# State-space phase of a four-layer kernel: smaller background products, at most one in a step

## The chip, the cores and the metric

The kernel runs on one core of one Trainium2 chip. The metric is the device time of one execution in microseconds (us), lower is better. The change touches the first of six phases, the program's first 4.49 ms.

## The reference, cut to what matters

The phase computes a 2-D selective state-space layer on four images of 48x48 positions and 128 channels: a layer norm, a projection to 2x256 channels, a depthwise 3x3 convolution with SiLU, four scans of the image (by rows and by columns, each forward and backward) and a gated projection back.

```python
xc = silu(conv3x3_depthwise(xc) + conv_b)            # 256 channels
xs = stack([x_hw, x_wh, x_hw[::-1], x_wh[::-1]])     # 4 orders of the 2304 positions
dts, Bs, Cs = split(x_proj_w @ xs)                   # 8 + 16 + 16 rows
delta = softplus(dt_w @ dts + dt_b)
# for each of 16 states n, along the positions t:
h = h * exp(delta_t * A[:, n]) + delta_t * u_t * B_t[n]
y_t += h * C_t[n]                                    # plus Ds * u
out = x + out_proj(layernorm(sum of 4 orders of y) * silu(z))
```

## The kernel before, in words

**Units and steps.** `layer0` (L112) cuts each of the 4 images x 4 passes into 5 chunks of 480, 480, 480, 480 and 384 positions. That makes 80 units (`units`), 20 to an image. In `units` an entry is (image b, o, d, chunk); o = 1 means that positions are read by columns, through a strided view. A unit has 16 steps, one for each state n, so the phase has 1280 steps g. Both halves of the 256 channels lie side by side, so one instruction does 2 x 480 elements.

**One order for all engines.** A planner in plain Python writes one list, `ph.order`, of named pieces of work. Each engine then walks this list and emits what is its own, in that order, with semaphore waits. So an engine never passes a piece that waits: whatever stands behind it waits too.

**The chain of a step.** For step g the list holds, in this order:

- `scan` g: VectorE's scan (L728), which needs `exp` g from ScalarE (L877, two halves; the second half of `exp` g+1 may start only when scan g has ended, since the three banks of `pA` are shared), `dbu` g from GpSimd (L941), and `add` g-4 (the buffer H has four places);
- `exp` g+1, and `carry` g (ScalarE, L885, waits for scan g);
- `c_spread` g-1 (TensorE): spreads row C of the state over 128 partitions in PSUM bank `pC`. There is one such bank, so it waits for `hc` g-2;
- `add` g-2 (TensorE, two products into `pY`). In the first step of a unit `add` waits until the previous unit's `pY` has been copied out (`y_out`, ScalarE, L894, put in step 1, right behind `add` of that unit's last step);
- `hc` g-1: VectorE's product of H with `pC` (L736), which needs `c_spread` g-1;
- `dbu` g+3 (GpSimd, up to three steps ahead).

**Work for the next unit.** `proj(u + 1)` is a Python generator; the loop advances it once in each step of unit u (`next(nxt, None)`). It puts `px` (TensorE, two products of 104 rows that give dts, B and C; ScalarE copies them out as `px_high` at L817 and `dts` at L821), `px_mid` and `px_low` (the rest of C's three bf16 parts), and for each half `dt`, `sp_exp`, `sp_ln`, `sp_max` and `du` (softplus; `sp_max` is VectorE's L719, `sp_ln` is ScalarE's L853 and L857). At step n = 12 (N - AHEAD - 1) whatever is left of it is put at once. `inject` (TensorE, step 9) adds the skip term or the earlier passes' sum into `pY`.

**Background work.** `todo` holds generators for other images: `front` (norm, the `in` and `z` products, the convolutions) and `back` (norm, gate and output projection of the image just finished). `further()` advances the first of them by one place. There is one place in a step, two in units 0 to 3 and, in the first pass of images 1 to 3 (`UB <= u and u % UB < 5`), two in every fourth step. A generator is held up where `take` finds neither of two free PSUM banks (`pM`), which `proj` and the background share. A convolution chunk of one channel half is nine TensorE products (taps), put as three pieces of three taps in three places (`conv` 0, 3, 6), then SiLU over five places. Where the chunk that the next unit reads is not ready (`ready_for`), the loop runs `further()` on the spot until it is.

The lines that matter: `take`, `conv`, `proj` and the step loop in the planner, L556 to L563 (`conv` on TensorE) and L589 to L596 (`px` on TensorE), L810 to L822 (`px` on ScalarE). All TensorE products share line L521 in the profile and are told apart by their tiles: `a_pC<-a_stk,a_sel` is `c_spread`, `a_pY<-a_H,cst` is `add`, `a_pM<-a_XC,a_w_x` is `px`, `a_pM<-a_xpad,a_cdiag` is `conv`, `a_pY<-a_Y,cst` is `inject` of a later pass. One fp32 product counts as two matmul instructions.

Of the kernel before, what the change touches and what calls it, by code (L numbers as in the profile page):

```python
# [111 lines left out]
def layer0(nc, A, X, K):  # L112
    ph = Phase(nc, "a")
# [105 lines left out]

    banks, freed, bank = [((), k) for k in range(8)], {}, {}  # L220

    def take(kind, *key):
        while not banks:
            yield
        freed[kind, key], bank[kind, key] = banks.pop(0)
        ph.put(kind, *key)

# [43 lines left out]
    def conv(b, h, c):  # L271
        yield from take("conv", b, h, c, 0)
        yield
        ph.put("conv", b, h, c, 3)
        yield
        ph.put("conv", b, h, c, 6)
        yield
        yield from silu("conv", b, h, c)
        give(("conv", (b, h, c, 0)), ("si_out", upto("si_out", "conv", b, h, c)))
        yield  # L280
# [52 lines left out]

    def proj(u):
        yield from take("px", u)
        ph.put("b_store", u)
        yield
        ph.put("px_mid", u)
        yield
        ph.put("px_low", u)  # L340
        give(("px", (u,)), ("px_low", u + 1))
        yield
        for h in range(2):
            k = 2 * u + h
            yield from take("dt", u, h)
            yield
            ph.put("sp_exp", u, h)
            yield
            ph.put("sp_ln", u, h)
            yield  # L350
            yield
            ph.put("sp_max", u, h)
            give(("dt", (u, h)), ("sp_max", k + 1))
            ph.put("du", u, h)
# [9 lines left out]

    def drain(target):
        for _ in target:
            pass

    def first_maps():
        yield from norm(0, 0, both)  # L370
# [16 lines left out]
    def further():  # L387

        while todo and next(todo[0], "end") == "end":
            todo.pop(0)  # L390
# [5 lines left out]
    def ready_for(u):  # L396

        b, o, d, ck = units[u]
        last = 4 if o or ck == 4 else ck
        return all(("si_out", ("conv", b, h, last)) in ph.rank for h in range(2))  # L400
# [13 lines left out]
    for g in range(G):  # L414
        u, n = divmod(g, N)
        if n == 0:
            b = u // UB
            if u % UB == 0:
                todo += ([back(b - 1)] if b else []) + ([front(b + 1)] if b + 1 < B else [])
            if u == NU - 5:  # L420
                todo.append(back(B - 1))
            if u + 1 < NU:
                while not ready_for(u + 1):
                    further()
            nxt = proj(u + 1) if u + 1 < NU else iter(())
        ph.put("scan", g)
        put_at("exp", g + 1)
        ph.put("carry", g)
        put_at("c_spread", g - 1)
        put_at("add", g - 2)  # L430
        put_at("hc", g - 1)
        put_at("dbu", g + AHEAD)
        if n == 1 and u:
            ph.put("y_out", u - 1)
        if n == 9:
            ph.put("inject", u)
        if (g + AHEAD) % 2:
            p = (g + AHEAD) // 2 + NB
            if p < G // 2:
                while ("b_store", (2 * p // N,)) not in ph.rank:  # L440
                    next(nxt)
                    further()
                ph.put("b_load", p)
        next(nxt, None)
        while n == N - AHEAD - 1 and next(nxt, "end") != "end":
            further()
        for _ in range(2 if u < 4 or UB <= u and u % UB < 5 and n % 4 == 3 else 1):
            further()
    ph.put("c_spread", G - 1)
    ph.put("add", G - 2)  # L450
# [1 line left out]
    ph.put("add", G - 1)  # L452
    ph.put("y_out", NU - 1)
    while todo:
        further()

    conv_ends = [key[:3] for kind, key in ph.order if kind == "conv" and key[3] == 6]
    conv_no = {key: k for k, key in enumerate(conv_ends)}

    def taken(kind, key):  # L460
# [18 lines left out]
    with nc.Block() as block:  # L479
# [38 lines left out]
        def _(pe):  # L518

            def mm(out, lhsT, rhs, start=True, stop=True):  # L520
                return pe.matmul(out, lhsT, rhs, start=start, stop=stop, skip_group_check=True)  # L521
# [11 lines left out]
            for kind, key in ph.order:  # L533
# [17 lines left out]
                elif kind == "conv":  # L551
# [4 lines left out]
                        wait_bank(kind, key)  # L556
                        pe.wait_ge(S("in_out"), upto("in_out", b, h, min(c + 1, 4)))
                    p = flat(taken("conv", (b, h, c, 0))[:, 0:z])
                    for t in range(t0, t0 + 3):
                        dy, dx = t // 3, t % 3  # L560
                        m = mm(p, cdiag[:, h, t, :], xpad[:, h, r0 + dy:r0 + dy + nr, dx:dx + 48], t == 0, t == 8)
                    if t0 == 6:
                        m.then_inc(S("conv"), 1)  # L563
                elif kind == "b_centre":
                    k = key[0]
# [23 lines left out]
                elif kind == "px":  # L589
# [3 lines left out]
                    for h in range(2):  # L593
                        pe.wait_ge(S("si_out"), upto("si_out", "conv", b, h, 4 if o else ck))
                    mm(p, w_x[:, 0, o + 2 * d, :], view(XC[:, b % 2, 0, :], o, ck), True, False)
                    mm(p, w_x[:, 1, o + 2 * d, :], view(XC[:, b % 2, 1, :], o, ck), False, True).then_inc(S(kind), 1)  # L596
                elif kind in ("px_mid", "px_low"):
                    u = key[0]
                    z = CHUNK[units[u][3]][1]
# [141 lines left out]
        def _(s):  # L741
# [4 lines left out]
            for kind, key in ph.order:  # L746
# [53 lines left out]
                elif kind == "b_rstd":  # L800
# [6 lines left out]
                    s.activation(rs[:, 0:BP], taken("b_var", key)[:, 0:BP], ACT.Ln, bias=K["eps5"]).then_inc(S("b_ln"), 1)  # L807
                    s.wait_ge(S("b_ln"), k + 1)
                    s.activation(rs[:, 0:BP], rs[:, 0:BP], ACT.Exp, scale=-0.5).then_inc(S(kind), 1)
                elif kind == "px":  # L810
                    u = key[0]
                    z = CHUNK[units[u][3]][1]
                    p = taken(kind, key)
                    s.wait_ge(S("px"), u + 1)
                    if u >= 2:
                        s.wait_ge(S("c_spread"), N * (u - 1))
# [2615 lines left out]
```

## Time and profile before

| | |
|---|---|
| three runs | 11725.56, 11732.56, 11735.66 us; median 11732.56 |
| profiled execution | 11683.06 us, span of its instructions 11681.3 us |
| mean granted TensorE clock | 0.936 of full speed |
| first scan to last product of the state-space phase | 119.9 to 4487.1 us |
| DVE in it | 4049.13 us busy of 4367 |
| TensorE in it | 3546.29 us busy, granted clock 0.98 |
| ScalarE, GpSimd in it | 2596.23 and 3570.75 us busy |

Times in the rows are microseconds from the start of the span. "Idle before" and the number in square brackets are the time for which that engine stood idle ahead of the instruction, with the work that ended it. PE is TensorE, DVE VectorE, ACT ScalarE, POOL GpSimd.

### The profile page before, as it was taken

The page shows a single profiled execution, that of the slowest core. Times are in us where ns is not written, and L with a number is a line of the kernel's source. Part 1 is how long each engine was busy: PE and PEld are TensorE (multiplying, and loading weights), DVE is VectorE, ACT ScalarE, POOL GpSimd, SP SyncE. Part 2 cuts the span into 40 slices and gives each one's busy share as a digit, 9 for nine tenths or more (in the row PEclk, how much of TensorE's full clock was granted, in tenths as well). Part 3 has the DMA queues.
Part 4 walks back from the last instruction along what each step waited for, and adds up shares of the span by engine and source line. Part 5 has one row for each costly group of instructions (what it writes and reads, how often), then busy time and mean ns, then how long its engine had stood idle before and what let it go on. Part 6 is the DMA issues. An engine that isn't in the chain of part 4 may idle for free. (4 is left out here: it accounts for less than half of the span.)

```text
span 11681.3 us, 158135 instructions
## 1 busy us (share of the span) xinstructions
PE 9607.7 (82%) x57482; PEld 5109.2 (44%) x57482; DVE 7460.1 (64%) x7471; ACT 5885.3 (50%) x11044; POOL 5628.1 (48%) x4841
## 2 busy tenths in 40 slices
PE   7788888888888776555499999999999998799996
PEld 3333333343333233444455555555555554333334
DVE  5999999999999995444455555454554543344532
ACT  4655565566555553111156666665665665233232
POOL 5888888878888885655432323222322220011010
PEclk9999999999999998888799999999999999899988
DMA  2222222222222224555400000000000001200003
GB/s 69 74 73 69 80 75 71 74 77 76 68 76 76 75 75 128 162 153 145 122 9 1 5 5 1 5 1 5 1 5 5 1 1 47 89 1 1 1 1 133
DMA packets 259800, 624.10 MB, mean 53 GB/s; under 512 B 26759, under 2 KB 115183, under 8 KB 256728
## 3 DMA queue, kind: packets, MB, share of 16 engines
q1 hardware_dynamic: 204696, 439.59, 11.5%
q0 software_dynamic: 51840, 169.91, 5.0%
q8 instruction: 467, 7.65, 0.3%
q10 hardware_dynamic: 2496, 4.49, 0.1%
q14 instruction: 301, 2.47, 0.1%
HBM read 572.72 MB, written 40.90 MB: 53 GB/s over the span
## 5 line engine op out<-in xcount | busy, mean ns | idle before, releaser
L941 POOL TENSOR_TENSOR a_dBu<-a_du,a_Bs 128x960 f32<-128x960 f32 (+1 forms) x1280 | 2743.4, 2144 | 0.6
L728 DVE TENSOR_TENSOR_SCAN a_H<-a_pA,a_dBu 128x962 f32<-128x962 f32 (+1 forms) x1280 | 2652.9, 2073 | 127.6 <-ACT a_pA L877 92.5
L521 PE MATMUL a_pY<-a_H,cst 128*128 128x480 f32 (+1 forms) x5120 | 2265.6, 565 | 62.3 <-ACT a_Y L894 62.2
L877 ACT ACTIVATE a_pA<-a_delta,a_al 128x480 f32<-128x480 f32 (+1 forms) x2560 | 1619.5, 638 | 1280.0 <-DVE a_H L728 1278.6
L736 DVE TENSOR_TENSOR a_H<-a_H,a_pC 128x960 f32<-128x960 f32 (+1 forms) x1280 | 1396.5, 1091 | 157.6 <-PE a_pC L521 155.9
L521 PEld LDWEIGHTS a_pY<-a_H,cst 128*128 128x128 f32 x5120 | 995.8, 197 | 758.9 <-issue 582.2
L1045 POOL DMA_INDIRECT b_gath<-b_tab,b_idx x648 | 730.3, 1127 | 500.3 <-PE b_pS L1096 269.7
L521 PE MATMUL a_pC<-a_stk,a_sel 96*128 96x480 bf16 (+1 forms) x1280 | 477.0, 373 | 560.5 <-DVE a_H L736 554.8
L1096 PE MATMUL b_pS<-cst,b_gath 128*128 128x128 f32 x2592 | 425.4, 342 | 584.0 <-DVE b_gath L1174 584.0
L2361 POOL TENSOR_TENSOR c_KF<-c_KF,c_dg 128x1056 f32<-128x1056 f32 x192 | 384.9, 2005 | 1045.0 <-DVE c_MX L2130 1043.8
L3286 POOL TENSOR_TENSOR e_P<-e_P 128x1024 f32<-128x1024 f32 (+1 forms) x80 | 151.7, 1917 | 1485.4 <-ACT e_P L3262 1485.4
L1170 DVE TENSOR_TENSOR b_gath<-b_gath,b_pW 128x4608 f32<-128x4608 f32 x72 | 356.7, 4954 | 661.8 <-ACT b_pW L1219 647.2
L3262 ACT ACTIVATE e_P<-e_slot 128x1024 f32<-128x1024 f32 (+1 forms) x464 | 347.5, 797 | 660.9 <-PE e_slot L3017 593.2
L1096 PEld LDWEIGHTS b_pS<-cst,b_gath 128*128 128x128 f32 x2592 | 413.7, 255 | 598.4 <-issue 598.4
L2201 DVE SCALAR_TENSOR_TENSOR X<-c_P,c_be,X 128x384 f32<-128x384 f32 x192 | 118.2, 615 | 862.9 <-PE c_P L1838 862.9
L521 PEld LDWEIGHTS a_pC<-a_stk,a_sel 96*128 96x128 bf16 x1280 | 125.6, 98 | 1237.3 <-DVE a_H L736 1081.4
L1838 PE MATMUL c_P<-c_un,c_W 128*128 128x384 f32 x1536 | 594.4, 511 | 44.7 <-ACT c_QFT L2292 30.7
L1838 PE MATMUL c_P<-c_U,c_W 128*128 128x384 f32 x1536 | 551.4, 511 | 40.7 <-DVE c_Mz L2181 30.7
L2313 ACT ACTIVATE c_G<-c_P,c_be 128x384 f32<-128x384 f32 x768 | 436.8, 582 | 206.0 <-PE c_P L1838 174.7
L1228 ACT ACTIVATE b_smp<-b_pS 128x512 f32<-128x512 f32 (+1 forms) x216 | 98.1, 488 | 875.5 <-PE b_pS L1096 875.5
L3165 DVE TENSOR_REDUCE e_part<-e_slot 128x2 f32<-128x1024 f32 (+3 forms) x400 | 417.1, 1068 | 168.5 <-PE e_slot L3017 162.5
L1838 PE MATMUL c_P<-c_G,c_W 128*128 128x384 f32 x1536 | 520.4, 492 | 0.2
(453 smaller groups left out, 17822.6 us busy)
## 6 DMA issues: line engine op xcount, KB each, us to landing
a_Bs<-a_brows SPq DMA_DIRECT2D x512, 480.0 KB, 3.6
a_Bs<-a_brows SPq DMA_DIRECT2D x128, 384.0 KB, 3.5
d_W<-in_d_w SPq DMA_DIRECT2D x32, 1024.0 KB, 8.1
f_W<-in_f_w SPq DMA_DIRECT2D x32, 1024.0 KB, 8.1
b_tab<-b_TT SPq DMA_DIRECT2D x32, 576.0 KB, 11.8
b_gath<-b_tab,b_idx POOLq DMA_INDIRECT x648, 3.7
a_zt<-a_sz SPq DMA_DIRECT2D x36, 256.0 KB, 3.6
a_sz<-a_zt SPq DMA_DIRECT2D x16, 480.0 KB, 4.0
```

Of the source, the lines that this page charges most:

```text
L521: return pe.matmul(out, lhsT, rhs, start=start, stop=stop, skip_group_check=True)
L728: v.tensor_tensor_scan(span(H[:, g % NH, :], g), factors(g), span(dBu[:, g % ND, :], g), 0.0, ALU.mult, ALU.add).then_inc(S(kind), 1)
L736: v.tensor_tensor(inner(H[:, g % NH, :], g), inner(H[:, g % NH, :], g), pC[:, 0:z].unsqueeze(1).broadcast_to([128, 2, z]), ALU.mult).then_ ...
L877: s.activation(pA[:, k, at:at + z], delta[:, u % 2, h, 0:z], ACT.Exp, scale=al[:, o + 2 * d, h, n:n + 1]).then_inc(S(kind), 1)
L941: g.tensor_tensor(inner(dBu[:, i % ND, :], i), du[:, u % 2, :, 0:z], Bs[:, p % NB, i % 2, 0:z].unsqueeze(1).broadcast_to([128, 2, z]), ALU ...
L1045: g.indirect_dma_start(out=gath[:, n % NG, t, :], out_offset=None, in_=tab[b], in_offset=bass.IndirectOffsetOnAxis(ap=idx[:, b % 2, j * 9 ...
L1096: m = pe.matmul(pS[:, place[kind, key], (t % 4) * 128:(t % 4 + 1) * 128], gath[:, n % NG, t, q * 128:(q + 1) * 128], ident, start=q == 0, ...
L1170: v.tensor_tensor(g, g, pW[:, n % 2, 0:36].unsqueeze(2).broadcast_to([128, 36, 128]), ALU.mult).then_inc(S("weighed"), 1)
L1838: return pe.matmul(out, lhsT, rhs, start=start, stop=stop, skip_group_check=True)
L2313: s.activation(G[:, c % 2, j, :], half("up", n, c // 2 * 2, 0)[:, j, 0:CH], ACT.Gelu, bias=bias(n, 5 + j)).then_inc(S(kind), 1)
L2361: g.tensor_tensor(KF[:, c, :, :, :], KF[:, c, :, :, :], dg[:, c % 2, :].rearrange("p (i g) -> p i g", i=4).unsqueeze(3).broadcast_to([128, ...
L3165: v.tensor_reduce(part[:, n % NR, i - 4 * j, 2 * hp:2 * hp + 2, kc], sl[:, :, 0:z], AX.X, ALU.max).then_inc(S(kind), 1)
```

## The change

The planner gets a flag, `crowded`. The loop clears it at the start of each step, except in step 9 (the step with `inject`), where it sets it. `take` (a bank for a first product) and the new `room` (a place for a further product) wait while it is set, and set it. It is cleared behind the `take` of a `dt`, before a second place in the same step, and wherever the planner is in a hurry.

- `conv` is put as five pieces, of 2, 2, 2, 2 and 1 taps, not three of three; a convolution's generator so takes eleven places, not nine.
- The two products of `px` are put in two steps: the second as `px_second`, and with it the ScalarE copies and `b_store`. The rest of `proj` comes one step later.
- In ScalarE's part (L810) the branch for `px` becomes that for `px_second`.
- In the first pass of images 1 to 3, there are two places in every odd step, not in every fourth: eight steps of a unit, not four.

```diff
+    crowded = [False]
+    def room():
+        while crowded[0]:
+            yield
+        crowded[0] = True
     def take(kind, *key):
-        while not banks:
+        while not banks or crowded[0]:
             yield
+        crowded[0] = True
...
     def conv(b, h, c):
         yield from take("conv", b, h, c, 0)
         yield
-        ph.put("conv", b, h, c, 3)
-        yield
-        ph.put("conv", b, h, c, 6)
-        yield
+        for t in range(2, 9, 2):
+            yield from room()
+            ph.put("conv", b, h, c, t)
+            yield
...
     def proj(u):
         yield from take("px", u)
+        yield
+        yield from room()
+        ph.put("px_second", u)
         ph.put("b_store", u)
...
             yield from take("dt", u, h)
+            crowded[0] = False
...
                 while not ready_for(u + 1):
+                    crowded[0] = False
                     further()
...
+        crowded[0] = n == 9
         next(nxt, None)
         while n == N - AHEAD - 1 and next(nxt, "end") != "end":
+            crowded[0] = False
             further()
-        for _ in range(2 if u < 4 or UB <= u and u % UB < 5 and n % 4 == 3 else 1):
+        for k in range(2 if u < 4 or UB <= u and u % UB < 5 and n % 2 else 1):
+            crowded[0] = crowded[0] and not k
             further()
...
-                    for t in range(t0, t0 + 3):
+                    for t in range(t0, min(t0 + 2, 9)):
...
-                    if t0 == 6:
+                    if t0 == 8:
...
-                    mm(p, w_x[:, 1, o + 2 * d, :], view(XC[:, b % 2, 1, :], o, ck), False, True).then_inc(S(kind), 1)
+                elif kind == "px_second":
...
+                    mm(flat(taken("px", key)[0:104, 0:CHUNK[ck][1]]), w_x[:, 1, o + 2 * d, :],
+                       view(XC[:, b % 2, 1, :], o, ck), False, True).then_inc(S("px"), 1)
...
-                elif kind == "px":
+                elif kind == "px_second":
...
-                    p = taken(kind, key)
+                    p = taken("px", key)
```

## Rows read from the trace of the kernel before

**Rows 1.** The page: busy time, share of the span and instructions of each engine.
```profile
PE 9607.7 (82%) x57482; PEld 5109.2 (44%) x57482; DVE 7460.1 (64%) x7471; ACT 5885.3 (50%) x11044; POOL 5628.1 (48%) x4841
```

**Rows 2.** Waits of DVE in the phase: us in total, times, longest us.
```profile
DVE a_H L736 <- PE a_pC L521: 155.3, 166, 3.4
DVE a_H L728 <- ACT a_pA L877: 92.5, 109, 2.5
DVE a_XC L698 <- ACT a_XC L794: 39.7, 5, 10.1
DVE a_H L728 <- PE a_pY L521: 16.5, 33, 1.4
```

**Rows 3.** Busy time by pass (80 steps each): us, engines, granted clock, DMA share, GB/s.
```profile
2879.50:3163.90 284.40, 239.75 (x560) 96.74 (x560) 254.33 (x180) 163.96 (x349) 225.44 (x199) 0.96 0.21 71
...
3713.60:3970.00 256.40, 194.14 (x470) 74.61 (x469) 247.36 (x170) 150.17 (x323) 215.12 (x195) 1.00 0.23 75
...
sum 4367.20, PE 3546.39 PEld 1515.08 DVE 4049.33 ACT 2596.23 POOL 3570.85; mean PE 221.65 PEld 94.69 DVE 253.08 ACT 162.26 POOL 223.18
```

**Rows 4.** Timeline, start of unit 67 (column pass, no background): start us, us, engine, line.
```profile
3819.58 2.15 DVE L728 TENSOR_TENSOR_SCAN a_H<-a_pA,a_dBu 128x962 f32<-128x962 f32 x1
...
3819.72 0.38 PE L521 MATMUL a_pC<-a_stk,a_sel 96*128 96x480 bf16 x1 [1.13 <-DVE a_H L736]
...
3821.55 3.38 PE L521 MATMUL a_pM<-a_XC,a_w_x 128*104 128x480 f32 x4
...
3822.70 2.15 DVE L728 TENSOR_TENSOR_SCAN a_H<-a_pA,a_dBu 128x962 f32<-128x962 f32 x1
...
3824.75 0.38 PE L521 MATMUL a_pC<-a_stk,a_sel 96*128 96x480 bf16 x1
...
3824.96 0.56 ACT L817 ACTIVATE a_stk<-a_pM 32x480 bf16<-32x480 f32 x1 [2.41 <-PE a_pM L521]
...
3825.17 1.16 DVE L736 TENSOR_TENSOR a_H<-a_H,a_pC 128x960 f32<-128x960 f32 x1 [0.32 <-PE a_pC L521]
...
3825.88 1.22 ACT L877 ACTIVATE a_pA<-a_delta,a_al 128x480 f32<-128x480 f32 x2
...
3826.68 0.40 PE L521 MATMUL a_pM<-a_stk,a_nsel 32*96 32x480 bf16 x1
...
3827.15 1.77 ACT L894 ACTIVATE a_Y<-a_pY 128x480 f32<-128x480 f32 x2
3827.31 2.16 DVE L728 TENSOR_TENSOR_SCAN a_H<-a_pA,a_dBu 128x962 f32<-128x962 f32 x1 [0.98 <-POOL a_dBu L941]
...
3830.84 2.16 DVE L728 TENSOR_TENSOR_SCAN a_H<-a_pA,a_dBu 128x962 f32<-128x962 f32 x1 [0.33 <-ACT a_pA L877]
```

**Rows 5.** Timeline, unit 30, steps 1 to 4: a convolution behind px.
```profile
1793.54 1.16 DVE L736 TENSOR_TENSOR a_H<-a_H,a_pC 128x960 f32<-128x960 f32 x1 [0.46 <-PE a_pC L521]
...
1798.30 1.15 DVE L736 TENSOR_TENSOR a_H<-a_H,a_pC 128x960 f32<-128x960 f32 x1 [1.53 <-PE a_pC L521]
...
1799.80 1.07 PE L521 MATMUL a_pM<-a_fb,a_w_dt 9*128 9x480 f32 x2
...
1800.80 2.68 PE L521 MATMUL a_pM<-a_xpad,a_cdiag 128*128 128x480 f32 x6
...
1803.72 1.16 DVE L736 TENSOR_TENSOR a_H<-a_H,a_pC 128x960 f32<-128x960 f32 x1 [2.20 <-PE a_pC L521]
```

**Rows 6.** Timeline, unit 67, step 10: behind inject.
```profile
3855.69 1.16 DVE L736 TENSOR_TENSOR a_H<-a_H,a_pC 128x960 f32<-128x960 f32 x1 [0.32 <-PE a_pC L521]
```

**Rows 7.** Timeline, end of unit 0: two convolutions on the spot.
```profile
172.96 14.65 PE L521 MATMUL a_pM<-a_xpad,a_cdiag 128*128 128x480 f32 x36
...
184.27 0.72 DVE L698 SCALAR_TENSOR_TENSOR a_XC<-a_pM,a_col,a_XC 128x480 f32<-128x480 f32 x1 [10.08 <-ACT a_XC L794]
```

**Rows 8.** Groups by line in the phase: count, busy us, mean ns, idle before.
```profile
L853 ACT ACTIVATE a_sp<-a_sp,a_less 128x480 f32<-128x480 f32 (+1 forms) x158 | 104.9, 664 | 0.0
L719 DVE SCALAR_TENSOR_TENSOR a_delta<-a_pM,a_delta 128x480 f32<-128x480 f32 (+1 forms) x158 | 99.2, 628 | 0.0
```

More of the change, by code:

```diff
@@ L366, in drain @@
         for _ in target:
-            pass
+            crowded[0] = False
     def first_maps():
@@ L440, in layer0 @@
                 while ("b_store", (2 * p // N,)) not in ph.rank:
+                    crowded[0] = False
                     next(nxt)
@@ L443, in layer0 @@
                 ph.put("b_load", p)
+        crowded[0] = n == 9
         next(nxt, None)
         while n == N - AHEAD - 1 and next(nxt, "end") != "end":
+            crowded[0] = False
             further()
-        for _ in range(2 if u < 4 or UB <= u and u % UB < 5 and n % 4 == 3 else 1):
+        for k in range(2 if u < 4 or UB <= u and u % UB < 5 and n % 2 else 1):
+            crowded[0] = crowded[0] and not k
             further()
@@ L454, in layer0 @@
     while todo:
+        crowded[0] = False
         further()
-    conv_ends = [key[:3] for kind, key in ph.order if kind == "conv" and key[3] == 6]
+    conv_ends = [key[:3] for kind, key in ph.order if kind == "conv" and key[3] == 8]
     conv_no = {key: k for k, key in enumerate(conv_ends)}
@@ L595, in _ @@
                     mm(p, w_x[:, 0, o + 2 * d, :], view(XC[:, b % 2, 0, :], o, ck), True, False)
-                    mm(p, w_x[:, 1, o + 2 * d, :], view(XC[:, b % 2, 1, :], o, ck), False, True).then_inc(S(kind), 1)
+                elif kind == "px_second":
+                    u = key[0]
+                    b, o, d, ck = units[u]
+                    mm(flat(taken("px", key)[0:104, 0:CHUNK[ck][1]]), w_x[:, 1, o + 2 * d, :],
+                       view(XC[:, b % 2, 1, :], o, ck), False, True).then_inc(S("px"), 1)
                 elif kind in ("px_mid", "px_low"):
```

## The prediction

> **What bounds the kernel now.** I read the page first, then the waits of DVE in the phase that the change touches, then its passes, then single steps. On the page no engine is near full over the whole span [rows 1], so the share of an engine says nothing until a stage is picked. The state-space phase takes 4367 us, 37% of the span, and there DVE is busy for 4049 us [rows 3]: it is the bound, and all that an order of work can win is what DVE stands idle, some 318 us. The waits name it: 155.3 us in L736 for `c_spread`, 92.5 us in L728 for `exp`, 16.5 us for `add`, and 39.7 us for SiLU where a convolution is done on the spot [rows 2].
>
> How a step without trouble runs: scans 0 and 1 of unit 67 start 3.12 us apart [rows 4]. TensorE starts `c_spread` 0.14 us behind the scan's start, and needs 1.83 us from there until the next product, `px`, starts (3819.72 to 3821.55) [rows 4]; this holds `c_spread` and both products of `add`. So 3.12 - 1.83 = 1.29 us of a step are free for other products. A step may be overdrawn, since `c_spread` is wanted only by L736, behind the 2.15 us scan. I call **lateness** the time from a scan's start to the start of its `c_spread`. In step 1 of unit 67 it is 3824.75 - 3822.70 = 2.05 us, and L736 waits 0.32 us for it [rows 4]; behind `inject` it is 0.32 us again [rows 6]. So about 1.75 us of lateness is borne without a wait, and what is above it is stalled. Lateness grows in a step by 1.83 + (the other products) - 3.12, and after a stall it counts as 1.75.
>
> Why background hurts: three taps take 2.68 us as recorded; with the 0.16 us by which each group's record overlaps the next it is about 2.5. Behind `px` (3.38 recorded, 3.20 from start to start [rows 4]) three such pieces made L736 wait 0.46, 1.53 and 2.20 us in steps 2 to 4 of unit 30, the last two with `dt` (1.00) between [rows 5]. That is 4.2 us for one half of one chunk.
>
> **Part 1, the convolution in five pieces.** No product is added. Of the 155.3 us, `px` and `inject` by themselves make about 0.32 us each in the 40 units of column passes: 80 x 0.32 = 26 us. I give some 27 us to the `back` products (no row shows them apart), which leaves 102 us for the 32 convolution halves that run inside the steps, 3.2 us each; the other eight of the 40 are ahead of the scans or on the spot. A piece of two taps takes 2.5 x 2/3 = 1.7 us. Lateness then grows by 1.83 + 1.7 - 3.12 = 0.41 a step: from 0.14 it reaches 1.78 after four pieces, no stall. Behind a split `px`, with `px_mid` and `px_low` (0.40 recorded, taken as 0.33 with the overlap [rows 4]) and a `dt`, I get 0.14, 0.45, 0.76, 1.5, 2.3, 3.2, 2.2, which stalls 0.55 + 1.45 + 0.4 = 2.4 us. Half of the halves behind `px`, half free: 1.2 us each. Saved: 32 x 2.0 = **64 us**. The ends are 0 (TensorE is full and only moves its stall) and 102 us (all of it).
>
> **Part 2, `px` in two steps.** In unit 67 `px` ended late, ScalarE's L817 waited 2.41 us for it, and `exp` of step 2, queued behind, ended at 3827.10, so scan 2 started 3827.31 - 3822.70 = 4.61 us behind scan 1, 1.49 us more than 3.12; the profile names POOL for this wait, but L877's end, 0.21 us before, fits the order. Then `y_out` (1.77 us) made scan 3 late by 3.53 - 3.12 = 0.41 us [rows 4]. With one product in step 0, `add` ends before it is wanted and `exp` 2 is on time: 1.9 us are gone. What is late next: `y_out`, L817 and L821 now stand together in step 1 of ScalarE's queue. Counted from scan 0: carry ends at 6.15, `y_out` 7.8, the two copies (0.56 and 0.54, less overlap) 8.75, two halves of `exp` 3 (1.22) 9.97, so scan 3 starts near 10.05, not 9.36: 0.7 us late. Net 1.2 us in 40 column units, 48 us; where a background ScalarE instruction also falls in steps 1 or 2 (0.6 to 1.3 us each) the gain is gone, and I take a third off: **32 us**. In row passes `px` is short and there is little to gain. The ends are -20 (ScalarE late every time) and 75 us (40 x 1.9).
>
> **Part 3, nothing beside `inject`.** Step 9 takes no background product. `inject` alone still overdraws by 0.32 us [rows 6]. A convolution piece beside it cost more, in few places: **8 us**, between 0 and 15.
>
> **Part 4, places.** A half takes two more places: ten halves, 20 places an image, and 20 are added (four in each of five units). `proj` and step 9 also close 3 of 16 steps for products. The front of an image must be ready when its units start; I count a delay of some 30 steps against a margin of 76 to the chunk that is wanted last (chunk 4 is read in the fifth unit). So nothing is forced. In units 0 and 1 the planner runs two halves on the spot now: TensorE 14.65 us, DVE idle 10.1 us before the first SiLU result [rows 7], 39.7 us in all [rows 2]. These stay, and with places lost before them one or two more products fall in: **-4 us**, between -15 and +5.
>
> **Part 5, `proj` one step later.** `sp_max` (0.63 us, L719 [rows 8]) and `du` of the second half come at step 12, not 11. GpSimd still has `dbu` 13 to 15 ahead, so nothing waits. But where a norm holds both banks in step 4, `dt` slips to 5, the second would come in step 9, is shut out until 10, and `sp_ln` and `sp_max` fall together in step 12: DVE then waits for carry (0.19) and two ScalarE instructions of 0.66 us [rows 8] behind the second `exp` half (0.65) less its own L736 (1.05), about 1.1 us. Six to eight such units: **-8 us**, ends 0 and -80. On SP the store comes a step later and its load is asked for in step 8, so the DMA is covered by seven steps, 22 us.
>
> **Sum.** 64 + 32 + 8 - 4 - 8 = 92; I add 8 for the `back` products, which now avoid some of `px`: **100 us**. Against the profiled execution, 11683.1 us, this gives 11583; the three runs have a median 49.5 us above it, and the difference is carried over: 11732.6 - 100 = 11632.6 us. Check by passes: column pass 10 takes 284.4 us with 254.3 busy on DVE, column pass 13, with no background, 256.4 with 247.4 [rows 3]. 30 us of idle against 9: the forecast takes 6.3 us off a pass on average and about 12 off such a one, so it does not take more than is there.
>
> **A rule against it.** Start to start, a change from one group of products to the next costs nothing that can be seen: `px` begins at 3821.55, the next `c_spread` at 3824.75, before the 3.38 us of `px` have passed [rows 4]. The Trainium skill ("TensorE: Matmul & The Clock Gate", "Single matmul latency") says that a matmul on its own costs (398 + N)/2.4 ns where one in a stream costs about N/2.4, so 0.17 us more. If each of the 64 + 80 new pieces paid that, by the page the sum would be an estimated 76 us, not 100. The row speaks for nothing, since the pieces follow the adds without a gap.
>
> **The rivals.** (A) *TensorE has no room*: in column passes with background TensorE is busy 239.8 of 284.4 us [rows 3], so smaller pieces only spread the same stall, and part 2 is partly eaten by ScalarE. For it: 84% busy, and idle TensorE time where SiLU has no product to put. Against: pass 13 shows 194 of 256. Parts 1 and 2 at a quarter to a half, 24 to 48 us: about 11695. Chance 0.20. (B) *It does not do what it says*: second places in a step and `dt` clear the flag, so two products still meet, and the order is much as before: 0 to 20 us, 11722. Chance 0.10. (C) *`proj` falls behind*: its first `take` or its `dt` slips in most units, since `room` and `take` wait for one another, and step 12 must put the rest at once. Price 1.1 us of DVE, 1.0 us of `dt` beside a piece. In all 80 units this is 168 us against the 100: 11800. It decides where more than 100/2.1 = 48 units slip; I expect 6 to 8, because background holds two banks only in norms. Chance 0.07. Forecast: 0.63.
>
> **How the numbers follow.** The predicted time is that of the forecast, 11633. Its own range by the bounds of parts 1 and 2 is 11560 to 11680. With (A), 11715 holds about 8 in 10. A measurement of this kernel can tell 0.2%, 23.5 us. Faster by more: the forecast's 0.63, all but a little of (A) 0.17, some of (B) 0.02: 0.82. Within it: 0.11. Slower: 0.07.
>
> **What would show it.** Right: `DVE a_H L736 <- PE` falls from 155 to some 70 us; L817's wait for `px` goes and scan 2 follows scan 1 by 3.12 us in units like 67, with scan 3 some 0.7 us late instead; a convolution half is four records of x4 and one of x2 in L521, not three of x6; the on-the-spot stretch stays. Wrong: L736's wait stays above 120 us (A); L728's wait for L877 grows beyond 92 (ScalarE took over); L719 waits for L857 (C).

## The result, and the profile after

The changed kernel takes 11627.65 us (median of six runs, 11615.68 to 11635.31); the kernel before took 11731.22 in six runs beside it. The ratio is 0.9913, with a 95% interval of 0.99 to 0.9926: 104 us faster, where 100 were forecast.

The profiled execution took 11635.31 us (span 11633.5), only 48 us less than the one of before. The first phase alone lost more. From its first scan to its last it takes 4268.9 us (120.7 to 4389.6), against 4365.0 (119.9 to 4484.9): 96 us less. What comes behind it, untouched by the change, took 7244 us in this execution and 7196 in that of before; over all the kernels profiled below it lies between 7188 and 7259. So the phase's own time is compared in what follows, and the ratios stand for the whole.

The page's line of the engines, which answers to [rows 1]:

```profile
PE 9595.3 (82%) x57482; PEld 5099.6 (44%) x57482; DVE 7453.2 (64%) x7471; ACT 5879.4 (51%) x11044; POOL 5631.2 (48%) x4841
```

The waits of DVE in the phase, as [rows 2] (us in total, times, longest us; L759 is L736 of before, L751 is L728, L721 is L698, L742 is L719, L880 is L857):

```profile
DVE a_H L759 <- PE a_pC L540: 118.1, 126, 3.3
DVE a_H L751 <- ACT a_pA L900: 42.9, 65, 2.0
DVE a_XC L721 <- ACT a_XC L817: 41.2, 5, 10.9
DVE a_delta L742 <- ACT a_delta L880: 11.1, 11, 1.2
DVE a_H L751 <- PE a_pY L540: 10.1, 22, 1.5
```

DVE's work is the same (the pass table below: 4043.55 us busy in the phase, 4049.33 before). What fell is its waiting: for `c_spread` from 155.3 to 118.1 us, for `exp` from 92.5 to 42.9, for `add` from 16.5 to 10.1. One wait is new, `sp_max` for `sp_ln`, 11 times, 11.1 us. TensorE runs the same products as well, and yet its busy time falls from 3546.39 to 3522.60 us: for part of the phase its clock is granted at half, and that part is shorter after the change (see below).

Busy time by pass, the same two passes as in [rows 3] and the sum:

```profile
2828.90:3096.30 267.40, 230.97 (x556) 93.34 (x556) 252.78 (x179) 165.40 (x352) 225.77 (x198) 0.98 0.23 74
...
3635.40:3885.00 249.60, 194.11 (x470) 74.07 (x470) 246.38 (x170) 149.96 (x324) 214.61 (x193) 1.00 0.23 76
...
sum 4272.30, PE 3522.60 PEld 1499.77 DVE 4043.55 ACT 2589.41 POOL 3576.57; mean PE 220.16 PEld 93.74 DVE 252.72 ACT 161.84 POOL 223.54
```

The column pass with background lost 17.0 us (284.4 to 267.4), the one without 6.8 (256.4 to 249.6). The second has no background work, so there only the split of `px` and the later `proj` can act; the first has the convolutions besides. The granted clock is full in the second both times. In the first it goes from 0.96 to 0.98: TensorE stood at half clock for 23.9 us of that pass before and for 10.2 after. DVE's waits for `c_spread` there fall from 13.2 to 4.5 us outside those stretches and stay inside them (5.6 and 6.1), so the clock doesn't explain them.

**By step of a unit.** I took for each step the time from scan to scan, less 3.12 us (2.575 in a unit of 384 positions), less 0.9 of the recorded time of DVE's other instructions in it: what is left is lost time. Summed over the 80 units, by the step's number:

| steps | before, us | after, us |
|---|---|---|
| 0 to 4 (`px`, `y_out`, the copies) | 209 | 71 |
| 5 to 8 | 37 | 41 |
| 9 and 10 (`inject`) | 39 | 75 |
| 11 and 12 | 7 | 16 |
| 13 to 15 (the on-the-spot stretches are in 15) | 45 | 38 |
| all | 338 | 242 |

So the change wins 138 us in the first five steps and gives 40 back between steps 5 and 10. No term of the prediction stands for that second number.

**Where it was won.** The timeline at the start of unit 67, the unit of [rows 4] (start us, us, engine, line):

```profile
3738.69 2.15 DVE L751 TENSOR_TENSOR_SCAN a_H<-a_pA,a_dBu 128x962 f32<-128x962 f32 x1
...
3740.66 1.77 PE L540 MATMUL a_pM<-a_XC,a_w_x 128*104 128x480 f32 x2
...
3741.80 2.15 DVE L751 TENSOR_TENSOR_SCAN a_H<-a_pA,a_dBu 128x962 f32<-128x962 f32 x1
...
3742.25 0.38 PE L540 MATMUL a_pC<-a_stk,a_sel 96*128 96x480 bf16 x1
...
3744.08 1.77 PE L540 MATMUL a_pM<-a_XC,a_w_x 128*104 128x480 f32 x2
...
3744.69 1.80 ACT L917 ACTIVATE a_Y<-a_pY 128x480 f32<-128x480 f32 x2
3744.92 2.16 DVE L751 TENSOR_TENSOR_SCAN a_H<-a_pA,a_dBu 128x962 f32<-128x962 f32 x1
...
3745.67 0.38 PE L540 MATMUL a_pC<-a_stk,a_sel 96*128 96x480 bf16 x1
3746.28 0.59 ACT L840 ACTIVATE a_stk<-a_pM 32x480 bf16<-32x480 f32 x1
...
3747.22 1.23 ACT L900 ACTIVATE a_pA<-a_delta,a_al 128x480 f32<-128x480 f32 x2
...
3748.64 2.16 DVE L751 TENSOR_TENSOR_SCAN a_H<-a_pA,a_dBu 128x962 f32<-128x962 f32 x1 [0.52 <-ACT a_pA L900]
```

Scans 0 to 2 start 3.11 and 3.12 us apart: scan 2 is on time (it was 4.61 us behind scan 1). Scan 3 comes 3748.64 - 3744.92 = 3.72 us later, 0.60 late: on ScalarE `y_out` (L917, 1.80 us) and the two copies stand ahead of `exp` 3 (L900 at 3747.22), as forecast. The halves of `px` cost 3742.25 - 3740.66 = 1.59 and 3745.67 - 3744.08 = 1.59 us from start to start, 3.18 together, against the 3.20 of one piece [rows 4].

**Where it was given back.** Unit 28, steps 6 to 11, a convolution behind the row-order `px`, and its last piece:

```profile
1675.51 1.77 PE L540 MATMUL a_pM<-a_xpad,a_cdiag 128*128 128x480 f32 x4
...
1677.12 0.37 PE L540 MATMUL a_pC<-a_stk,a_sel 96*128 96x480 bf16 x1
...
1683.46 2.15 DVE L751 TENSOR_TENSOR_SCAN a_H<-a_pA,a_dBu 128x962 f32<-128x962 f32 x1
...
1683.60 1.07 PE L540 MATMUL a_pM<-a_fb,a_w_dt 9*128 9x480 f32 x2 [1.07 <-DVE a_delta L742]
...
1684.60 1.88 PE L540 MATMUL a_pM<-a_xpad,a_cdiag 128*128 128x480 f32 x4
...
1686.31 0.37 PE L540 MATMUL a_pC<-a_stk,a_sel 96*128 96x480 bf16 x1
...
1686.72 1.16 DVE L759 TENSOR_TENSOR a_H<-a_H,a_pC 128x960 f32<-128x960 f32 x1 [1.10 <-PE a_pC L540]
...
1688.13 1.77 PE L540 MATMUL a_pY<-a_Y,cst 128*128 128x480 f32 x4
...
1691.56 0.97 PE L540 MATMUL a_pM<-a_xpad,a_cdiag 128*128 128x480 f32 x2
```

The half is four records of x4 and one of x2, as announced (two of the four are shown). A piece of two taps takes 1677.12 - 1675.51 = 1.61 us, and in steps 5 to 7 no piece makes DVE wait. Then comes the second half's `dt`, which is in step 8 of the list. It needs a bank that `sp_max` (L742) frees at the end of that step, so it starts at 1683.60, 0.14 us behind the next scan; since its `take` clears the flag, a piece of convolution stands right behind it. `c_spread` comes 1686.31 - 1683.46 = 2.85 us behind its scan, and L759 waits 1.10 us. In unit 31, step 10, a column unit, `inject` then follows:

```profile
1850.63 2.15 DVE L751 TENSOR_TENSOR_SCAN a_H<-a_pA,a_dBu 128x962 f32<-128x962 f32 x1
1850.97 3.38 PE L540 MATMUL a_pY<-a_Y,cst 128*128 128x480 f32 x4
...
1854.17 0.38 PE L540 MATMUL a_pC<-a_stk,a_sel 96*128 96x480 bf16 x1
...
1854.59 1.16 DVE L759 TENSOR_TENSOR a_H<-a_H,a_pC 128x960 f32<-128x960 f32 x1 [1.81 <-PE a_pC L540]
```

`c_spread` starts 1854.17 - 1850.63 = 3.54 us behind its scan, and DVE waits 1.81. Before, `dt` stood in step 7, a step further from `inject`. DVE's waits for TensorE in steps 9 and 10 went from 37 to 67 us, in steps 1 to 4 from 97 to 22, in steps 5 and 6 from 9 to 32.

**Where the clock stood at half.** What stands beside `inject` isn't the only thing that changed there. The trace records the clock granted to TensorE, and in this phase it has two levels, 1.00 (2.4 GHz) and 0.50 (1.2 GHz). Two stretches of unit 27 (start and end, length, busy time of PE, PEld, DVE, ACT and POOL, granted clock, DMA share, GB/s), and `inject` in the second:

```profile
1620.00:1632.00 12.00, 7.67 (x20) 3.00 (x19) 11.71 (x9) 7.76 (x16) 8.82 (x8) 1.00 0.29 91
1632.00:1635.00 3.00, 3.00 (x5) 1.23 (x4) 3.00 (x3) 2.53 (x6) 3.00 (x5) 0.50 0.38 137
```

```profile
1633.18 2.89 PE L540 MATMUL a_pY<-a_Y,cst 128*128 128x480 f32 x4
```

TensorE was busy for 7.67 of the 12 us before the clock fell. `inject` takes 2.89 us there and L759 waits 0.78 us behind it, with no convolution piece ahead. In unit 28, where TensorE was busy for 10.93 of the 12 us from 1676 to 1688, the clock stays at 1.00 and `inject` takes 1.77 us (above). In the whole phase TensorE stood at half clock for 193 us before the change and for 143 after.

I sorted DVE's waits for `c_spread` by the products that stand ahead of it in its step, and by whether the clock stood at half for part of that step (the sums are 0.2 and 0.3 us above those of the waits, since the ends of the phase are cut a little differently):

| ahead of `c_spread` | before, us | of it at half clock | after, us | of it at half clock |
|---|---|---|---|---|
| a convolution piece | 88.2 | 7.0 | 44.5 | 15.3 |
| `inject`, no convolution | 25.5 | 18.1 | 49.3 | 31.2 |
| others (`px`, `dt`, `back`) | 41.8 | 15.6 | 24.6 | 2.0 |
| all | 155.5 | 40.7 | 118.4 | 48.6 |

The fall of this wait lies at full clock (114.8 to 69.8 us). Of the 36 us that steps 9 and 10 lose more (the table by step), 24 stand in steps in which the clock was at half for a part (14.9 to 39.1), and 11 in the others (24.7 to 36.0). So two causes meet there, the second `dt` with a piece beside it ahead of `inject`, and `inject` at half clock. No run changed the clock alone, so their shares aren't shown.

The new wait of L742, unit 26, step 12, where `sp_ln` (its second instruction, L880, 0.68 us from 1589.06) and `sp_max` share a step:

```profile
1589.78 0.66 DVE L742 SCALAR_TENSOR_TENSOR a_delta<-a_pM,a_delta 128x480 f32<-128x480 f32 x1 [0.98 <-ACT a_delta L880]
```

And the end of unit 0 is as it was in [rows 7], two convolutions on the spot, TensorE 14.65 us on them again and DVE idle for 10.88 before the first SiLU result:

```profile
184.68 0.72 DVE L721 SCALAR_TENSOR_TENSOR a_XC<-a_pM,a_col,a_XC 128x480 f32<-128x480 f32 x1 [10.88 <-ACT a_XC L817]
```

### The profile page after: what moved, and what is told of

Read it like the earlier page. It is cut to its first block and busy times, and to the rows that moved or that the text cites. A ratio compares the mean times of both kernels' runs of the same rounds, so it can differ in the third digit from the quotient of the medians.

```text
span 11633.5 us, 158135 instructions
## 1 busy us (share of the span) xinstructions
PE 9595.3 (82%) x57482; PEld 5099.6 (44%) x57482; DVE 7453.2 (64%) x7471; ACT 5879.4 (51%) x11044; POOL 5631.2 (48%) x4841
## 5 line engine op out<-in xcount | busy, mean ns | idle before, releaser
L751 DVE TENSOR_TENSOR_SCAN a_H<-a_pA,a_dBu 128x962 f32<-128x962 f32 (+1 forms) x1280 | 2656.7, 2076 | 63.2 <-ACT a_pA L900 42.9
L900 ACT ACTIVATE a_pA<-a_delta,a_al 128x480 f32<-128x480 f32 (+1 forms) x2560 | 1623.8, 639 | 1380.9 <-DVE a_H L751 1379.8
L540 PE MATMUL a_pY<-a_H,cst 128*128 128x480 f32 (+1 forms) x5120 | 2239.5, 559 | 31.5 <-ACT a_Y L917 31.2
L759 DVE TENSOR_TENSOR a_H<-a_H,a_pC 128x960 f32<-128x960 f32 (+1 forms) x1280 | 1399.1, 1093 | 119.1 <-PE a_pC L540 118.5
L1861 PE MATMUL c_P<-c_U,c_W 128*128 128x384 f32 x1536 | 555.0, 514 | 40.8 <-DVE c_Mz L2204 30.8
```

What stands on the lines that cost most here:

```text
L751: v.tensor_tensor_scan(span(H[:, g % NH, :], g), factors(g), span(dBu[:, g % ND, :], g), 0.0, ALU.mult, ALU.add).then_inc(S(kind), 1)
L759: v.tensor_tensor(inner(H[:, g % NH, :], g), inner(H[:, g % NH, :], g), pC[:, 0:z].unsqueeze(1).broadcast_to([128, 2, z]), ALU.mult).then_ ...
L900: s.activation(pA[:, k, at:at + z], delta[:, u % 2, h, 0:z], ACT.Exp, scale=al[:, o + 2 * d, h, n:n + 1]).then_inc(S(kind), 1)
```

## The experiments

**The table.** Ratio to the kernel before, with its interval; the phase from first to last scan; lost time in the sense of the table above; and DVE's waits for `c_spread` and for `exp`, from the waits of each profile. All but the ratio is of one execution each.

| kernel | ratio [95%] | phase, us | lost, us | for `c_spread` | for `exp` |
|---|---|---|---|---|---|
| before | 1 | 4365.0 | 338.2 | 155.3 | 92.5 |
| changed | 0.9913 [0.99, 0.9926] | 4268.9 | 241.7 | 118.1 | 42.9 |
| before_px_split | 0.9958 [0.9944, 0.9972] | 4324.7 | 297.0 | 149.3 | 61.1 |
| before_conv_pieces | 0.9956 [0.9939, 0.9972] | 4331.2 | 304.2 | 142.1 | 69.6 |
| after_px_whole | 0.9942 [0.9926, 0.9959] | 4302.3 | 275.4 | 116.5 | 64.8 |
| after_conv_three | 0.9944 [0.9927, 0.996] | 4303.0 | 276.2 | 145.1 | 57.0 |
| after_no_flag | 0.9914 [0.9896, 0.9931] | 4275.4 | 247.3 | 125.5 | 51.6 |
| after_places_old | 0.9918 [0.9901, 0.9935] | 4272.3 | 245.5 | 109.5 | 51.8 |
| after_inject_11 | 0.9921 [0.9905, 0.9938] | 4269.3 | 242.1 | 96.6 | 70.2 |
| after_copies_late | 0.9883 [0.9866, 0.9899] | 4220.7 | 193.3 | 103.4 | 8.4 |
| after_no_idle_place | 0.9921 [0.9904, 0.9937] | 4292.1 | 264.3 | 148.7 | 47.1 |
| after_both_moves | 0.9846 [0.983, 0.9863] | 4182.7 | 155.3 | 75.2 | 16.5 |
| both_moves_early_places | 0.984 [0.9824, 0.9857] | 4189.8 | 162.7 | 83.2 | 19.6 |

### Each of the two splits alone

before_px_split: the kernel before, with `px` in two steps.

```diff
         yield from take("px", u)
+        yield
+        ph.put("px_second", u)
         ph.put("b_store", u)
...
```

> The kernel before, with px alone put in two steps (second product, ScalarE copies and b_store one step later, all behind it one step later); convolutions stay three pieces of three taps, no flag. Theory P (two mechanisms: the split px frees exp of step 2, the smaller pieces free c_spread): the wait of L728 for exp falls from 92.5 us to 40 to 60, that of L736 for c_spread by 10 to 30 from 155; but dt of the second half now stands in step 8, right ahead of inject, which costs some 10 to 25 us back. About 40 us faster, ratio 0.9965. Rival S (smaller pieces alone do it): ratio 1.000. Rival X (the split px alone does it): ratio 0.991.

before_conv_pieces: the kernel before, with the convolution in five pieces.

```diff
-        ph.put("conv", b, h, c, 3)
-        yield
-        ph.put("conv", b, h, c, 6)
-        yield
+        for t in range(2, 9, 2):
+            ph.put("conv", b, h, c, t)
+            yield
...
```

> The kernel before, with convolutions alone put as 2, 2, 2, 2 and 1 taps; px whole, no flag. Theory P: pieces still fall beside px, inject and dt, so L736's wait for c_spread falls only from 155 to 110 to 130 us, L728's for exp stays near 90. About 30 us faster, ratio 0.9975. Rival S: 0.991. Rival X: 1.000.

Measured: 0.9958 and 0.9956, in the phase 41 and 34 us less lost time (338.2 - 297.0, 338.2 - 304.2). The waits of DVE, first with `px` split, then with the convolution in pieces:

```profile
DVE a_H L734 <- ACT a_pA L883: 61.1, 72, 2.1
```

```profile
DVE a_H L735 <- PE a_pC L520: 142.1, 161, 3.1
DVE a_H L727 <- ACT a_pA L876: 69.6, 109, 1.8
```

The split of `px` takes its gain from the wait for `exp` (92.5 to 61.1, a little less than expected); `c_spread` gives 6 us where 10 to 30 were expected. The pieces take theirs from both waits, 13 us from `c_spread` (25 to 45 were expected) and 23 from `exp`, which was expected to stay near 90; that `exp` is late where TensorE was late fits this but wasn't traced. So the two waits aren't two parts of the change, one each, and the pieces alone gained more than the 0.9975 expected.

### Each of the two splits taken out of the changed kernel

after_px_whole puts `px_second` in the step of `px`; after_conv_three goes back to three pieces of three taps.

```diff
-        yield
-        yield from room()
         ph.put("px_second", u)
```

> The changed kernel with px in one step again (both products, copies and b_store in step 0), the flag and the small convolution pieces kept. Theory P: scan 2 is late by 1.5 us again in column passes (L728's wait for exp near 90 us), while scan 3 is on time and dt leaves inject's side: about 30 to 45 us of the 103 are lost, ratio to the kernel before 0.9945. Rival S: 0.991. Rival X: 1.000.

```diff
-        for t in range(2, 9, 2):
+        for t in (3, 6):
...
-                    for t in range(t0, min(t0 + 2, 9)):
+                    for t in range(t0, t0 + 3):
...
-                    if t0 == 8:
+                    if t0 == 6:
```

> The changed kernel with convolutions as three pieces of three taps, everything else kept. Theory P: L736's wait for c_spread goes from 118 us to 140 to 165; L728's stays at 43. Ratio to the kernel before 0.9945. Rival S: 1.000. Rival X: 0.991.

Measured: 0.9942 and 0.9944; the lost time rises by 34 us each (275.4 and 276.2 against 241.7). In the time, each split is worth 0.0029 to 0.0044 of 11731 us, 34 to 52 us, and the two alone, 0.0042 + 0.0044, make up the 0.0087 of the change. In the traces they make up 41 + 34 = 75 of 96 us; single traces don't tell whether the other 21 are more than noise. Both mechanisms are real, neither needs the other for its gain, and their sizes can't be told apart within the intervals. The waits came less well than the ratios: with `px` whole `exp` waits 64.8 us, not 90, and with three taps it rises to 57.0, where 43 was expected; `c_spread` came at 145.1, as expected. And one thing bears on steps 9 and 10: with `px` whole the second `dt` is back in step 7, a step from `inject`, and yet these steps lose 70 us, against 75 in the changed kernel and 39 before.

### The flag and the places

after_no_flag: `take` and `room` no longer wait for `crowded`.

```diff
-        while not banks or crowded[0]:
+        while not banks:
...
-        while crowded[0]:
+        if False:
             yield
```

> The changed kernel with the flag without effect: take and room never wait for it; px in two steps, five convolution pieces and all places kept. What the flag is worth: the two parts alone gave 41 and 34 us in their profiles, the whole 96, so theory P expects about 20 us less gain than the changed kernel, ratio to the kernel before 0.993, with L736's wait at 130 to 145 us. Rival F (keeping products apart is the whole of the gain, the small pieces only allow it): ratio 0.998 or more.

after_places_old: two places in every fourth step again.

```diff
-        for k in range(2 if u < 4 or UB <= u and u % UB < 5 and n % 2 else 1):
+        for k in range(2 if u < 4 or UB <= u and u % UB < 5 and n % 4 == 3 else 1):
```

> The changed kernel with second places in every fourth step of a first pass, as before, not in every odd one. Theory: the pieces of back are held up by the two banks, not by places, so the added 20 places an image give nothing: within 10 us of the changed kernel, ratio to the kernel before 0.991. Rival: the places keep the norm's and gate's products off px, without them first passes lose 5 us each, ratio 0.9925.

Measured: 0.9914 and 0.9918, inside the interval of the changed kernel. In the trace they lose 5.6 and 3.8 us more, too little to call. The 20 us that I expected of the flag aren't there. Without it products do meet: L759 waits in nine steps behind `inject` and a convolution piece (24.3 us) and in nine behind `px` and a piece (10.5), and in the changed kernel in none; but the waits elsewhere are smaller by about as much, and `sp_max` no longer waits for `sp_ln`. The added places don't bring the convolutions forward: in both traces every SiLU result of a convolution comes in the same step. That the generators are held up by banks instead is argued, not shown.

### What was late next: `inject` and the copies

after_inject_11: `inject` two steps further from the second `dt`.

```diff
-        if n == 9:
+        if n == 11:
             ph.put("inject", u)
...
-        crowded[0] = n == 9
+        crowded[0] = n == 11
```

> The changed kernel with inject (and the step that the flag closes for it) at step 11, not 9. Theory D: the changed kernel loses some 30 us because dt of the second half, which now stands in step 8 and waits there for sp_max at the step's end, delays the start of inject; the wait of L736 in steps 9 and 10 (67 us in the changed kernel, 37 before) falls to 10 to 25 us. 25 to 45 us faster than the changed kernel, ratio to the kernel before 0.988. Rival E (inject's own length of 3.38 us makes that wait, wherever it stands): no change against the changed kernel, 0.991.

Measured: 0.9921, nothing gained. In steps 9 and 10 the waits for TensorE do go, from 67 to 9 us. The steps with `inject` (and no convolution) wait 11.1 us, not 49.3, and none of that stands at half clock any more, where 31.2 us did: the move takes `inject` away from `dt` and from the stretches at half clock alike, so it doesn't part the two causes. DVE's waits as a whole:

```profile
DVE a_H L759 <- PE a_pC L540: 96.6, 136, 3.1
DVE a_H L751 <- ACT a_pA L900: 70.2, 86, 2.5
```

The wait for `exp` is 27 us longer (in step 3 alone 50 instead of 25 us), and in steps 4 and 5 DVE waits 51 us for TensorE instead of 21. In unit 28 the convolution's first piece stands in step 4 now, not in 5, beside the first `dt`:

```profile
1651.66 2.15 DVE L751 TENSOR_TENSOR_SCAN a_H<-a_pA,a_dBu 128x962 f32<-128x962 f32 x1
...
1651.67 1.07 PE L540 MATMUL a_pM<-a_fb,a_w_dt 9*128 9x480 f32 x2
...
1652.67 1.88 PE L540 MATMUL a_pM<-a_xpad,a_cdiag 128*128 128x480 f32 x4
...
1654.38 0.37 PE L540 MATMUL a_pC<-a_stk,a_sel 96*128 96x480 bf16 x1
...
1654.79 1.16 DVE L759 TENSOR_TENSOR a_H<-a_H,a_pC 128x960 f32<-128x960 f32 x1 [0.98 <-PE a_pC L540]
```

A `dt` and a piece behind it again, 1654.38 - 1651.66 = 2.72 us, 0.98 waited, and from a lateness that is full DVE waits 0.20 for each further piece. The collision of a `dt` with a piece moved from step 8 to step 4, and took the slack of the later pieces with it. So the stall at `inject` is real, but moving `inject` alone isn't a cure. The wait for `exp` grew mostly in ten units, the first passes of images 2 and 3, where scan 3 waits 20.3 us in total and 1.3 in the changed kernel; why wasn't followed up.

after_copies_late: ScalarE's copies of `px` one step behind `px_second`, with one idle place of `proj` taken out, so that its end stays.

```diff
         ph.put("px_second", u)
+        yield
+        ph.put("px_copy", u)
         ph.put("b_store", u)
...
             ph.put("sp_ln", u, h)
             yield
-            yield
...
-                elif kind == "px_second":
+                elif kind == "px_copy":
```

> The changed kernel with ScalarE's two copies of px (px_high, dts) and b_store one step later than the second product, in step 2, and px_mid and px_low behind them; the idle place between sp_ln and sp_max is left out, so that the rest of proj ends no later. Theory Q: y_out and the two copies in one step make scan 3 late by 0.6 us in column passes; with the copies apart L728's wait for exp falls from 43 us to 10 to 20, 25 to 40 us faster than the changed kernel, ratio to the kernel before 0.988. Rival: y_out alone (1.77 us) makes it late, no change, 0.991.

after_no_idle_place: only the idle place taken out.

```diff
             ph.put("sp_ln", u, h)
             yield
-            yield
```

> The changed kernel with the idle place between sp_ln and sp_max left out, the copies of px where they are. It parts the two edits of the kernel with late copies, which was 0.0029 of the time before faster than the changed one. If late copies are the cause, this brings nothing for L728 (its wait for exp stays at 40 to 55 us), and moves dt of the second half from step 8 to 7, off inject: 0 to 15 us faster, ratio 0.9905. If the missing place is the cause: 0.988.

Measured: 0.9883 with the copies late, 0.9921 without. The waits of DVE with the copies late:

```profile
DVE a_H L760 <- PE a_pC L541: 103.4, 120, 3.0
...
DVE a_delta L743 <- ACT a_delta L881: 28.2, 16, 2.3
...
DVE a_H L752 <- ACT a_pA L901: 8.4, 19, 0.9
```

The wait for `exp` is all but gone, 42.9 to 8.4 us; in unit 67 the scans start at 3696.16, 3699.28, 3702.40, 3705.51 and 3708.63, none late. Taking out the idle place by itself gained nothing, against the 0 to 15 us expected: the ratio is within the interval of the changed kernel, the trace loses 23 us more, and the wait for `c_spread` rises from 118.1 to 148.7 us. With the second `dt` in step 7 again steps 9 and 10 lose 47 us and not 75, but steps 5 to 8 lose 78 instead of 41, and steps 0 to 4 92 instead of 71: the stall moved. The wait for `exp` stayed at 47.1, so its fall to 8.4 is the copies'. Whether their 48 us of lost time need the missing place as well is open, since no run had late copies with the place kept. The price is `sp_max` waiting for `sp_ln` in 16 units, 28.2 us.

after_both_moves is the edits of two kernels together, after_copies_late's and after_inject_11's.

> Both moves of the two kernels before this one together: inject in step 11, the copies of px in step 2. If the two causes are apart, the gains add: 50 to 80 us faster than the changed kernel, ratio to the kernel before 0.985. If TensorE is simply full, the second move brings nothing: 0.988.

Measured: 0.9846, 79 us below the changed kernel (11548.39 against 11627.65), and 86 us less lost. Here `inject` in step 11 is worth 38 us (193.3 to 155.3), where alone it was worth nothing. What goes is the wait for `c_spread` of the steps in which `inject` ran and the clock stood at half for a part (33.3 to 0.6 us). So here too it's open how much the clock did. The waits of DVE with both moves:

```profile
DVE a_H L760 <- PE a_pC L541: 75.2, 103, 2.8
...
DVE a_H L752 <- ACT a_pA L901: 16.5, 28, 1.5
```

both_moves_early_places adds to it places in units 0 and 1, four in a step, against the bursts on the spot.

```diff
-        for k in range(2 if u < 4 or UB <= u and u % UB < 5 and n % 2 else 1):
-            crowded[0] = crowded[0] and not k
+        for k in range(4 if u < 2 else 2 if u < 4 or UB <= u and u % UB < 5 and n % 2 else 1):
+            crowded[0] = crowded[0] and not k % 2
```

> The kernel with both moves (inject in step 11, copies of px in step 2), and four places a step in units 0 and 1, not two, the flag cleared before every second one. The convolutions on the spot at the ends of units 0 and 1 cost some 17 us each in the two traces; with more places all but little of image 0's front is ready in time, and its work runs beside the scans at the price of some stalls in 32 steps. Theory: 15 to 30 us faster than with both moves alone, ratio to the kernel before 0.9828. Rival (TensorE is full in those units and the work only stalls elsewhere): no gain, 0.9846.

Measured: 0.984, not to be told from 0.9846. The two stretches on the spot go (34.1 to 1.2 us of lost time), but the first five units lose 58 us instead of 39: their TensorE work and SiLU chains wait in the steps instead. The waits of DVE in those units, L722 for SiLU and L760 for `c_spread`:

```profile
DVE a_XC L722 <- ACT a_XC L818: 40.3, 5, 10.5
DVE a_H L760 <- PE a_pC L541: 3.8, 4, 1.4
```

```profile
DVE a_H L760 <- PE a_pC L541: 22.2, 18, 4.6
DVE a_XC L722 <- ACT a_XC L818: 21.2, 7, 6.5
```

So more places in units 0 and 1 don't help: the work must be done there anyhow, and on the spot or in the steps it costs about the same. These two are the best kernels of the study, and both beat the changed kernel.

## Why the prediction was right, and where it wasn't

The sum was right: 100 us forecast, 104 by the medians, 96 by the phase's trace. Its parts were not, and that the total hit is in part luck. The two main terms, 64 and 32, came out about equal, at 34 and 41 alone: 75 in place of 96. What the traces show beyond them, some 21 us, no run puts down to a term of the prediction.

**Part 1, the pieces: over-sized.** 64 us forecast; 34 in the trace, alone and taken out, 36 to 52 by the ratios. A piece's length was right (1.7 forecast, 1.61 measured), and so was the rule for a stall: 2.85 - 1.10 and 3.54 - 1.81 give 1.75 and 1.73 us of lateness borne without a wait, the 1.75 of the prediction. What failed is "I get 0.14, 0.45, 0.76, 1.5, 2.3, 3.2, 2.2": that row of steps put the pieces right behind `px`, ending before step 8. In units like 28 and 31 they begin in step 5, run free, and meet the second `dt` and `inject`; in units like 27 and 30 they begin behind `inject`, and DVE waits 0.20 us for each of the first two. The table by products tells the size. The waits in steps with a convolution piece fell from 88.2 to 44.5 us, by 44. For 32 halves that is 2.8 us each before and 1.4 after, where the prediction had 3.2 and 1.2. The first was too large, since `px` and `inject` by themselves made 39 us (13.3 and 25.5), not 26; the 27 us for `back` were right (28.5, without `px`). And `inject`, which the prediction left as it was, went from 25.5 to 49.3 us and took 24 of the 44 back. The sign announced, L736's wait at some 70 us, so didn't come: it is 118.1.

**Part 2, `px`: the size right.** 32 us forecast; 41 alone and 34 taken out, in the trace. Scan 2 is on time: its waits for `exp`, 58.6 us before, are gone. But 21.7 of them were in 21 row units, for which the prediction had "little to gain". Scan 3 is 0.60 late in unit 67, where 0.7 was forecast, and its waits for `exp` come to 25.0 us, 20.1 of them in 29 of the 40 column units. The third taken off for background on ScalarE was an estimate that no run separates.

**Part 3, nothing beside `inject`: not seen.** 8 us forecast. Without the flag the kernel is the same within the interval. The flag kept background products out of step 9, but `dt` and a piece from step 8 ran over into it, since the `take` of `dt` clears it. I had counted that clearing only for rival (B).

**Part 4, places: right.** Nothing was forced, the bursts on the spot stayed (34.9 us lost after, 33.5 before), and in images 2 and 3 the last SiLU result of a convolution comes 21 steps later in the trace (16 in image 1), within the 30 forecast.

**Part 5, `proj` a step later: right in kind.** 6 to 8 units at 1.1 us; 11 units at 0.8 to 1.2 us of wait, 11 us instead of 8, and none without the flag. But "so nothing waits" overlooked what else moved with it: the second `dt` came next to `inject`. That is the step of the prediction that failed, and units 28 and 31 show its cost at full clock. That all of the 30 us more in steps 9 and 10 hang on it isn't shown: with `px` whole and `dt` in step 7 these steps lose nearly as much, and 24 of the 36 us of lost time stand at half clock. The clock, 0.96 and 1.00 in the two passes of [rows 3], has no term in the prediction at all.

**The rivals.** (A), TensorE without room, named as its sign that L736's wait stays above 120 us. It stood at 118.1, and yet the time was not (A)'s: the total of one wait didn't tell a stall that stayed from one that went in one place and grew in another. The wait by steps would have. As a price (A) fell too: it gave both parts together 24 to 48 us, and alone they made 75. (B) fell as a forecast, since both splits do what they say; its mechanism, that `dt` clears the flag and two products still meet, is there in 22 steps with 30.8 us of waits. (C) fell: 11 units slipped, not 48.

**The rule on single matmuls.** The halves of `px` cost 3.18 us and the whole 3.20. The Trainium skill ("TensorE: Matmul & The Clock Gate", "Single matmul latency") gives (398 + N)/2.4 ns for a single bf16 matmul. If each new piece had paid the constant of that formula, it would have cost an estimated 0.17 us more; in this order, where a piece follows other products at once, the trace shows none of it.

## What to carry to other kernels

When work moves in a fixed order, write down for each moved piece what it will stand next to, and which buffer's release lets it start: a product that waits for a bank is late by the time of whoever frees it, and drags the next along. Sum a wait by its place in the loop, not only by its line, since a total can stand still while a stall moves. Look up the granted clock of the places where a stall grew before you give it to a neighbour in the order. And try the follow-up moves in pairs: `inject` two steps later was worth nothing alone and 38 us once the copies had been moved.

## What the runs showed of the hardware

Here an operand read by columns takes TensorE nearly twice as long as one read by rows. `inject` has the same form in both kinds of unit (`a_pY<-a_Y,cst`, 128x480, x4): 1.77 us in unit 28, which reads by rows, 3.38 in unit 31, which reads by columns, both at a granted clock of 1.00. `y_out` shows it too on ScalarE, whose output is that view: 1.80 us for the two instructions in unit 67 (column order, above), and in unit 28 (row order):

```profile
1660.22 1.01 ACT L917 ACTIVATE a_Y<-a_pY 128x480 f32<-128x480 f32 x2
```

In the column view neighbours are 48 fp32 elements apart. The Trainium skill ("SBUF — State Buffer", "Door 1: The DMA port swizzle") says that consecutive accesses to the same 16-byte line run at full bandwidth and that each one that crosses to a new line pays a penalty, for which it gives no figure; these pairs agree with it, 1.9 times for `inject` and 1.8 for `y_out`. No run here varied the stride, so how the cost grows with it is open.
